# A two-layer attention network on one core: evacuations in another order, three score products beside a V tile, and small VectorE operations with one input

## The reference

```
# layer 0
x = x + conv_attn(gn(x))       # qkv = gn(x) @ qkv_w + b;  softmax(q k^T * scale + rel_h + rel_w) v;  @ proj_w + b
# layer 1
t = tokens(x)
t = t + attn(ln(t))            # causal softmax(q k^T / sqrt(64)) v;  @ Wo + bo
t = t + ffn(ln(t))             # gelu(t @ kron(c_fc_1, c_fc_2).T) @ kron(c_proj_1, c_proj_2).T
# ln(v) = (v - mean) / sqrt(var + 1e-5)
```

## Time and profile before

| | us |
|---|---|
| median of 3 runs (lowest, highest) | 2788.88 (2784.71, 2790.33) |
| the profiled execution | 2787.91 |
| its span | 2786.2 |
| PE busy | 2597.0 (93%) |
| ACT busy | 1996.5 (72%) |
| DVE busy | 1907.6 (68%) |
| POOL busy | 1680.8 (60%) |

### The profile page before, as it was taken

How to read it: one execution, slowest core, us unless ns; L and a number is a source line. 1 busy time by engine, 2 the same in 40 slices (tenths; PEclk the granted TensorE clock), 3 DMA queues, 4 the chain that set the end, 5 groups by cost and what they waited for, 6 DMA issues and landing times.

```text
span 2786.2 us, 69295 instructions
## 1 busy us (share of the span) xinstructions
PE 2597.0 (93%) x29061; PEld 1540.1 (55%) x29061; DVE 1907.6 (68%) x3554; ACT 1996.5 (72%) x2387; POOL 1680.8 (60%) x1151
## 2 busy tenths in 40 slices
PE   7899999999999999999999999999998999999996
PEld 4465645656456564565645656466564655546563
DVE  8775757667676767757667576675776758677574
ACT  6686867858578595785867867678667777678684
POOL 5474756747567384683756747567465665747464
PEclk8999999999999999999999999999999999999998
DMA  3100012000110002000020000300003000110000
GB/s 110 40 2 2 2 33 72 2 1 2 48 57 2 1 2 76 28 2 1 2 84 21 2 1 2 103 2 2 1 8 97 2 2 2 24 58 2 2 2 24
DMA packets 52278, 64.50 MB, mean 23 GB/s; under 512 B 8672, under 2 KB 46176, under 8 KB 51968
## 3 DMA queue, kind: packets, MB, share of 16 engines
q1 hardware_dynamic: 50208, 59.66, 7.1%
q10 hardware_dynamic: 1760, 0.41, 0.1%
HBM read 30.75 MB, written 12.58 MB: 16 GB/s over the span
## 4 chain that ended last, share of the span: by engine, by line
PE 45%; POOL 17%; ACT 13%; DVE 13%; issue 11%; DMA 0%; SPq 0%; POOLq 0%; ACTq 0%; DVEq 0%
POOL pl L1139 16%; PE ps L571 9%; PE ps L1022 7%; PE ps L802 5%; PE ps L979 4%; PE ps L992 4%; PE ps L941 4%; ACT p L1073 4%; DVE mxp L1097 3%; PE ps L981 3%; ACT ph L1053 3%; DVE stats L1255 2%; DVE x L1251 2%; ACT qa L740 2%; PE ps L1230 2%
## 5 line engine op out<-in xcount | busy, mean ns | idle before, releaser
L1139 POOL TENSOR_TENSOR pl<-p,ph 128x1024 f16<-128x1024 f32 (+2 forms) x672 | 1095.9, 1644 | 366.8 <-ACT ph L1053 360.7
L1097 DVE TENSOR_REDUCE mxp<-ps 128x1 f32<-128x512 f32 (+2 forms) x1344 | 783.6, 626 | 265.4 <-PE ps L941 261.9
L1073 ACT ACTIVATE p<-ps 128x1024 f32<-128x1024 f32 (+1 forms) x672 | 640.3, 953 | 171.9 <-PE ps L992 171.1
L1053 ACT ACTIVATE ph<-p 128x1024 f16<-128x1024 f32 (+1 forms) x672 | 669.3, 996 | 21.4
L1022 PEld LDWEIGHTS ps<-v,ph 128*128 128x128 f16 x9600 | 506.2, 97 | 128.2 <-issue 27.5
L1022 PE MATMUL ps<-v,ph 128*128 128x65 f16 (+1 forms) x9600 | 531.1, 194 | 17.0 <-POOL pl L1139 16.5
L1022 PE MATMUL ps<-v,pl 128*128 128x65 f16 x4800 | 509.2, 192 | 0.0
L1022 PEld LDWEIGHTS ps<-v,pl 128*128 128x128 f16 x4800 | 446.7, 99 | 0.0
L992 PE MATMUL ps<-qc,kc 65*128 65x512 f16 (+3 forms) x1344 | 380.1, 364 | 0.0
L1139 DVE TENSOR_TENSOR pl<-p,ph 128x512 f16<-128x512 f32 (+1 forms) x336 | 243.9, 726 | 183.8 <-ACT ph L1053 182.8
L820 POOL TENSOR_TENSOR v<-o,v 128x384 f16<-128x384 f32 x128 | 115.7, 921 | 309.8 <-ACT o L816 309.3
(11 more groups left out here) (197 smaller groups left out, 4664.1 us busy)
## 6 DMA issues: line engine op xcount, KB each, us to landing
xin<-in_x SPq DMA_DIRECT2D x8, 1536.0 KB, 6.8
x<-in_x SPq DMA_DIRECT2D x8, 1536.0 KB, 6.8
out<-x SPq DMA_DIRECT2D x16, 768.0 KB, 3.6
qc<-qa SPq DMA_DIRECT2D x42, 128.0 KB
qa<-qa SPq DMA_DIRECT2D x21, 128.0 KB
qb<-qb SPq DMA_DIRECT2D x21, 128.0 KB, 2.4
qa<-o SPq DMA_DIRECT2D x56, 48.0 KB
qb<-o SPq DMA_DIRECT2D x56, 48.0 KB, 2.0
```

Source lines behind the costliest of these rows:

```text
L1053: self.nc.scalar.activation(m.ph[:, i % RING, :, 0:w], m.p32[:, i % RING, :, 0:w], ACT.Copy).then_inc(self.s["hi"], 1)
L1073: nc.scalar.activation(m.p32[:, i % RING, :, 0:w], m.ps[:, 2 * (i % 2):2 * (i % 2) + 2, 0:w], ACT.Exp, scale=SCALE).then_inc(s["exp"], 1)
L1097: nc.vector.reduce_max(m.mxp[:, h % 2, kh, qt:qt + 1], m.ps[:, bank, 0:w], AX.X).then_inc(s["free"], 1)
L1139: engine.tensor_tensor(m.pl[:, i % RING, part, 0:w], m.p32[:, i % RING, part, 0:w], m.ph[:, i % RING, part, 0:w], ALU.subtract).then_inc(s ...
```

## The change

Five edits:

1. In the feed-forward part VectorE does `o2_out(0)` between the two evacuations of key pair 3 instead of behind both.
2. ScalarE empties V tile 1 of the next image (`v_high(1)`) ahead of the last two relative-position copies instead of behind them.
3. The row of head 0 is followed by three products for maxima of head 1, each ahead of a third of the last V tile. TensorE's wait for the low parts of the relative positions moves ahead of them. The other 13 are spread over steps 0 to 4.
4. `combine` is a maximum over one input (`mxp` read as tile by half) that writes a new tensor `top`, instead of a maximum of two inputs written in place. Products that have one half only, in the causal layer, write `top` at once.
5. `eps` is a sum over pairs (variance, 1e-5) in `mv`, which has a third column for it, filled once by GpSimd, instead of an addition of a constant.

```diff
     def early(self, i):
-        return [u for u in self.uses_at[i][:2] if u[0] == "max" or u == ("row", 0)]
+        return [u for u in self.uses_at[i][:2 + (len(self.beside_row) if i == 0 else 0)] if u[0] == "max" or u == ("row", 0)]
...
-            steps[0].append(("row", 0))
+            self.beside_row = [("max", 1, n) for n in range(NC_)]
+            steps[0] += [("row", 0)] + self.beside_row
...
-                for n in range(self.NTL):
-                    steps[begin + n * (end - begin) // self.NTL].append(("max", h, n))
+                ahead = len(self.beside_row) if h == 1 else 0
+                for n in range(ahead, self.NTL):
+                    steps[begin + (n - ahead) * (end - begin) // (self.NTL - ahead)].append(("max", h, n))
...
-            nc.vector.reduce_max(m.mxp[:, h % 2, kh, qt:qt + 1], m.ps[:, bank, 0:w], AX.X).then_inc(s["free"], 1)
+            to = m.mxp[:, h % 2, kh, qt:qt + 1] if qt >= self.both.start else m.top[:, h % 2, qt:qt + 1]
+            nc.vector.reduce_max(to, m.ps[:, bank, 0:w], AX.X).then_inc(s["free"], 1)
...
-        nc.vector.tensor_tensor(m.mxp[:, h % 2, 0, both], m.mxp[:, h % 2, 0, both], m.mxp[:, h % 2, 1, both], ALU.max).then_inc(s["combined"], 1)
+        nc.vector.reduce_max(m.top[:, h % 2, both], m.mxp[:, h % 2, :, both].rearrange("p k t -> p t k"), AX.X).then_inc(s["combined"], 1)
...
-        self.nc.vector.tensor_scalar(self.m.ln[:, 0, t], self.m.mv[:, t, 1], 1e-5, None, ALU.add).then_inc(self.s["eps"], 1)
+        self.nc.vector.reduce_sum(self.m.ln[:, 0, t], self.m.mv[:, t, 1:3], AX.X).then_inc(self.s["eps"], 1)
...
             def beside_row():
 
-                qkv0.v_products(pe, NT - 1)
                 qkv0.rel_lows_ready(pe)
+                for c in range(NC_):
+                    attn0.use(pe, attn0.beside_row[c])
+                    qkv0.v_products(pe, NT - 1, [c])
...
                 w.next.qkv0.v_high(act, 0)
-                for r in range(12, 16):
+                for r in range(12, 14):
+                    w.next.qkv0.rel_high(act, r)
+                w.next.qkv0.v_high(act, 1)
+                for r in range(14, 16):
                     w.next.qkv0.rel_high(act, r)
...
-            low(3)
+            low(3, (0,))
             ff.o2_out(dve, 0)
+            low(3, (1,))
             ff.widen(dve, 0)
```

More of the change, by code:

```diff
@@ L106, in allocate @@
     m.stats = sb("stats", [P, NT, 6], F32)
-    m.mv = sb("mv", [P, NT, 2], F32)
+    m.mv = sb("mv", [P, NT, 3], F32)
     m.gstats = sb("gstats", [P, 2, 6], F32)
@@ L113, in allocate @@
     m.mxp = sb("mxp", [P, 2, 2, NT], F32)
+    m.top = sb("top", [P, 2, NT], F32)
     m.minus = sb("minus", [P, P], F32)
@@ L293, in gpsimd @@
         fill(m.minus_half[:, :], -0.5)
+        fill(m.mv[:, :, 2], 1e-5)
         fill(self.anti, 0.0)
@@ L853, in __init__ @@
         steps = [[] for _ in range(self.N)]
+        self.beside_row = []
         if self.causal:
@@ L945, in use @@
             pe.wait_ge(s["combined"], s.at("combined", h + 1))
-            mm = nc.tensor.matmul(m.ps[0:NT, bank, 0:P], m.mxp[:, h % 2, 0, :], m.minus[:, :], start=True, stop=True, skip_group_check=True)
+            mm = nc.tensor.matmul(m.ps[0:NT, bank, 0:P], m.top[:, h % 2, :], m.minus[:, :], start=True, stop=True, skip_group_check=True)
         elif u[0] == "unit":
@@ L1033, in tensor @@
                 for u in self.early(i):
-                    if u != ("row", 0):
+                    if u != ("row", 0) and u not in self.beside_row:
                         self.use(pe, u)
@@ L1258, in aggregate @@
         dve.wait_ge(self.s["stats"], self.s.at("stats", t + 1))
-        self.nc.vector.bn_aggr(self.m.mv[:, t, :], self.m.stats[:, t, :]).then_inc(self.s["mv"], 1)
+        self.nc.vector.bn_aggr(self.m.mv[:, t, 0:2], self.m.stats[:, t, :]).then_inc(self.s["mv"], 1)
     def eps(self, dve, hf):
@@ L1649, in scalar @@
             for t in range(NT):
-                if t > 0 or not before:
+                if t > 1 or not before:
                     qkv0.v_high(act, t)
```

## The result

| | before | after |
|---|---|---|
| median, us (lowest, highest) | 2789.61 (2784.71, 2791.53) | 2756.7 (2754.96, 2757.74) |
| span of the profiled execution, us | 2786.2 | 2754.4 |

The ratio is 0.9884, with a 95% interval of 0.9867 to 0.9901. The change makes the kernel 32.9 us faster; 29.5 were forecast, and 2756.7 lies in the range of 2753 to 2771. Each experiment has its own numbers, a few lines off.

A forecast was written before the change was run, and what follows sets the result against it. TensorE, busy 93% of the span, was taken as the bound, so its idle time counts. Seams 11.6, first attentions 16.3, first image 0.8 and last 0.8 sum to 29.5 us: 2759 forecast, range 2753 to 2771.

The forecast's parts named there:

- edit 1, per seam: Ahead of the first spread: the copy moves into VectorE's idle place and TensorE's wait goes, 1.0 us, bounds 0 and 1.1.
- edit 2, per seam: Wait at V tile 3 goes, about 1.0 returns at V tile 4; VectorE's first maximum comes 0.47 us earlier, bounds 0 and 0.54.
- edit 5, per seam: Feed-forward input in seven images: only TensorE's wait ahead of the first feed-forward product goes, 0.19 us.
- edits 3 and 4, per image: First attention: fewer maxima in steps 0, 2 and 4 win 1.13 us, the combine no longer waiting for GpSimd 1.2.
- first image: First attention's 2.33 us won, less 1.5 because the low-part wait now stands ahead of V tile 7, which covered it.
- last image: Feed-forward input, where VectorE is the chain: edit 5's 0.8 us counts whole.
- The rival on the seam: V tile 4 and VectorE are later, or the spread meets a Gelu; the seam gives its gain back: 2769, chance 0.11.
- edit 3's gain turns into other waits: First attention: TensorE runs into ScalarE or step 3's bank, losing 1.13 us per image: 2768, chance 0.13.
- the one-input forms wait: Combine and epsilon on VectorE still wait for GpSimd despite one input: 2771, chance 0.04.
- Slower: First attention: VectorE's two-input low parts collide with GpSimd's and stretch: 2795, chance 0.04.
- no change: GpSimd's low parts set the attention's pace, and all but about 3 us is taken back there: 2785, chance 0.03.
- the 337.5 that would have refuted me: Sign for the whole: images 336 us apart instead of 339.9; the forecast is wrong if they keep more than 337.5.

The follow-up runs named there:

- the fastest kernel: Changed kernel with five maxima of head 1 beside V tile 7, counts 2, 2, 2, 3, 2, and V tile 7 ahead of the first image's wait: 2748.00 us.
- four maxima: Changed kernel with four maxima of head 1 beside V tile 7, the others 2, 2, 2, 3, 3 over steps 0 to 4: 2754.40 us.
- five maxima: Changed kernel with five maxima of head 1 beside V tile 7, the others 2, 2, 2, 3, 2 over steps 0 to 4: 2751.78 us.
- four, counts 2, 2, 3, 3, 2: Changed kernel with four maxima of head 1 beside V tile 7, the others 2, 2, 3, 3, 2 over steps 0 to 4: 2756.05 us.

## Why the prediction was right, step by step

The direction, the place of each gain and the size of the whole held. Where the sizes were off:

| term | forecast, us | measured, us |
|---|---|---|
| edit 1, per seam | 1.0 | 1.24 |
| edit 2, per seam | 0.47 | 0.56 |
| edit 5, per seam | 0.19 | 0.36 |
| edits 3 and 4, per image | 1.13 + 1.2 = 2.33 | 2.37 |
| first image | +0.8 | -0.62 |
| last image | 0.8 | 0.8 |

**The seam.** Forecast 11.6; measured (1.51 + 0.68) x 7 = 15.3. The forecast was 3.7 too low, and edit 1 came out above its upper bound of 1.1. I took the bracketed wait as the gain in edits 1 and 5. Since TensorE's ends are modelled, the bracket is a lower bound, and the stretches to the spread came out 0.15 and 0.17 shorter than it; the 0.10 that edit 1 wins behind the spread was in no term, and no run says which wait it is. Edit 2's is not the wait that went (1.67 to 0.91 is 0.76), but what VectorE allowed, as the prediction chose: its idle time of 0.52 ahead of the first maximum is gone. The rival on the seam is refuted by the stretches.

**Edits 3 and 4.** The sum held, 7 x 2.37 = 16.6 against 16.3, and so did edit 3's terms, one by one. The length of each step is the distance between the first products with low queries of two steps (L981, L986), in the fifth image:

| | before | after | change | forecast |
|---|---|---|---|---|
| row of head 0 to step 0 | 2.01 | 2.65 | +0.64 | +0.65 |
| step 0 | 3.29 | 2.69 | -0.60 | -0.60 |
| step 1 | 2.69 | 2.69 | 0 | 0 |
| step 2 | 2.69 | 1.73 | -0.96 | -0.96 |
| step 3 | 2.75 | 2.76 | +0.01 | 0 |
| step 4 | 2.69 | 2.47 | -0.22 | -0.22 |
| step 5, with the row of head 1 | 4.13 | 2.89 | -1.24 | -1.2 |

What did not hold is the attribution of the last term. The prediction gave the 1.2 of `combine` to its one-input form. The kernel with edit 3 alone, and the one with all edits and a two-input `combine`, both have the 2.37. So the 1.2 goes by either of two edits: by the form (edit 4 alone, 1.18) or by the place (edit 3 alone). I had noted that `combine` "stands a maximum and a low part earlier", and did not lay the new place against GpSimd's operations. The time of the whole change, which has both edits, could not show this. The rivals that edit 3's gain turns into other waits and that the one-input forms wait are both refuted, by steps 3 to 5 above and by at most 172 ns.

The Trainium skill ("SBUF — State Buffer", Who interferes with whom) says that on trn2 `tensor_reduce` never contends with GpSimd for the port pair, and that an operation of VectorE with two SBUF inputs does. The runs agree with both halves: 96 combines and 32 epsilons with one input at 161 to 172 ns, and the two-input form at the same place in the program at up to 1.08 us.

**The first image.** This is the step that failed: +0.8 forecast, -0.62 measured. "V tile 7, which it covered" held: the low queries come 2.71 behind the row of head 0 in both kernels (99.73 less 97.01, the start of the row; 98.13 less 95.42), and TensorE, with nothing to do but the row, stood 2.33 of them. What I left out is the clock behind that pause (windows 95.40:98.10, 98.10:101.30 and 101.30:104.00 of the changed kernel; the last but two columns is the granted clock):

```profile
95.40:98.10 2.70, 0.40 (x3) 0.10 (x2) 2.18 (x3) 0.87 (x2) 0.88 (x1) 0.95 0.00 1
98.10:101.30 3.20, 3.17 (x10) 1.35 (x11) 1.38 (x2) 0.00 (x0) 0.00 (x0) 0.50 0.00 0
101.30:104.00 2.70, 2.38 (x12) 0.97 (x10) 1.19 (x2) 1.59 (x3) 0.89 (x1) 1.00 0.34 42
```

For 3.2 us TensorE is granted 1.2 GHz, after 2.7 us in which it was busy 0.4. The three maxima and the V tile take from 98.13 to 101.78, thus 3.65 instead of the forecast's 0.65 + 1.5 = 2.15: 1.5 us, which makes up the error of 1.4. With the V tile ahead of the wait, in the fastest kernel, the clock stays up:

```profile
95.80:98.50 2.70, 1.98 (x12) 0.90 (x11) 2.18 (x3) 1.55 (x4) 0.89 (x1) 1.00 0.00 1
98.50:101.70 3.20, 2.16 (x8) 0.71 (x9) 2.73 (x5) 0.19 (x1) 0.89 (x1) 1.00 0.83 231
```

The traces of all 14 kernels agree on this. The mean granted clock over the 3.2 us from the end of the wait for the low queries:

| V tile 7 | wait | kernels | granted clock | first image's stretch |
|---|---|---|---|---|
| behind the wait | 2.33 | changed kernel | 0.51 | 21.39 |
| | | two-input combine | 0.58 | 21.54 |
| | | four maxima | 0.59 | 20.89 |
| | | five maxima | 0.59 | 20.41 |
| | | edit 3 alone | 0.50 | 22.72 |
| | | four, counts 2, 2, 3, 3, 2 | 0.50 | 22.37 |
| ahead of the wait | 0.41 to 0.77 | the eight others | 1.00 | 18.77 to 20.78 |

In the last two with the long wait the clock was at 1.2 GHz already as the row of head 0 went out and did not rise through the pause; in the other four it fell during the pause or within 0.6 us of its end. So in every kernel with the pause TensorE works at 1.2 GHz behind it, and in none without. That the pause is the reason is the likeliest reading and not shown by itself: the runs varied the order of V tile and wait, not the pause alone.

**What was not in the sum.** The one-input `combine` costs a little elsewhere: the stretch from the row of head 5 to the causal layer is 80.14 at its lowest with edit 4 in and 80.06 without it, in seven images (the last has 78.64 in both): 0.08 x 7 = 0.6. From head 1 to head 5 it wins as much (90.60 instead of 90.68), at head 4's `combine`.

**The sum as measured:** 15.3 + 16.6 - 0.6 + 0.8 + 0.6 - 0.6 = 32.1. The span is 31.8 shorter: the first image's row of head 0 starts 1.6 earlier (95.42 instead of 97.01), the last image's transposes to the spread take 0.8 less (16.75 instead of 17.54, where the 14 kernels lie between 16.45 and 17.66), and stretches at a lower clock (below) take 2.7 more. The median is 32.9 lower. That the total came within 3.4 of the 29.5 has some luck in it, for the seam was 3.7 too low and the first image 1.4 too high.

**Slower and no change.** GpSimd's low parts did not take the gain back. From the second image on, images are 335.2 to 336.5 apart, below the 337.5 that would have refuted me. The mechanism of the slower rival exists, and appears as soon as more maxima leave the first steps.

## What to carry to other kernels

- Before you pay for a new form of an instruction that waits for another engine, look at where the same instruction will stand after the other edits. Two edits that each remove one wait are worth the wait once.
- Work shifted into the idle time of an evacuating engine pays until a two-input operation of that engine comes to lie beside GpSimd. Try the neighbouring counts: here that point showed in no row of the trace of before, only in the run with four.
- Compare start times from mark to mark. An edit worth 0.1% was plain in its stretch in every image, and lost in the medians.
- A wait moved ahead of the work that covered it costs that work's time, and may cost the clock of what follows: here 1.5 us each.

## What the runs showed of the hardware

**The granted clock varies at one place of the program.** Between the attention and the causal layer TensorE's clock is granted below full in some images, and not the same ones in each trace. The changed kernel, third and fourth image (windows: start and end, length, busy time of PE, PEld, DVE, ACT, POOL with counts, granted clock, DMA share, GB/s):

```profile
900.00:920.00 20.00, 17.90 (x186) 11.77 (x185) 12.51 (x35) 7.32 (x10) 6.50 (x5) 1.00 0.01 2
920.00:930.00 10.00, 9.60 (x48) 5.13 (x47) 3.85 (x7) 5.64 (x10) 6.39 (x2) 0.83 0.01 2
```

```profile
1256.00:1266.00 10.00, 9.29 (x53) 5.14 (x52) 3.85 (x7) 6.24 (x11) 6.57 (x2) 1.00 0.01 2
```

In the third image the mean over 10 us is 0.83, so TensorE is granted 1.2 GHz instead of 2.4 for about a third of them; ahead of it, it was busy 17.9 of 20 us. In the fourth it isn't. The stretch is then 81.01 instead of 80.14. In the profiled executions 2 of 8 images were longer in this way before, 4 after, 6 with edit 2 alone, 3 in the fastest kernel and none with five maxima (2744.2 us of span). At 0.7 to 1.5 us each that moves a run by several us, as much as edits 2 and 5 are worth. The changed kernel has one more such stretch in the seam ahead of the sixth image (0.83 from 1757 to 1767 us, 1.2 us lost). Of 18 runs of the kernel before in one series, the shortest (2784.03) had a mean granted clock of 0.990 and the longest (2793.88) one of 0.984. In all five kernels with a single edit the median fell 1.1 to 2.2 us less than the stretches add up to; they have 3 to 6 longer images, and whether that is chance is not shown.

**The start varies too.** The first image's row of head 0 started between 93.11 and 97.45 us, in kernels whose program up to there is the same or nearly so.
